# A decoder layer on one Trainium2 core: one copy frees the shared PSUM bank of cross-attention, its users are placed in other steps, context loads go to ScalarE's queue, and one-hot rows are made by wide operations

## The chip, the core and the metric

The kernel runs on one core of a Trainium2 chip. A core has TensorE (PE, matmuls and transposes), VectorE (DVE), ScalarE (ACT), GpSimd (POOL) and SyncE (SP, which here only issues DMAs). Each runs its own instructions in order, and they wait for one another through semaphores. SBUF and PSUM have 128 partitions, and PE writes only to PSUM. The metric is the device time of one execution in microseconds (us); lower is better.

## The reference

A pre-norm decoder layer in f32: `x` is (4, 512, 512) and the context (4, 512, 512).

```python
x = x + attention(layernorm(x), W_qkv, W_out, b_out)       # 16 heads of 32, rotary, window of 128
x = x + cross(layernorm(x), context, Wq, Wk, Wv)
x = x + experts(layernorm(x), router, gate, up, down)      # 64 experts, top 8, capacity 256

# cross: 32 heads of 16
q = rmsnorm(heads(x @ Wq.T)); k, v = heads(context @ Wk.T), heads(context @ Wv.T)   # interleaved in one kv
k = rmsnorm(k)
out = softmax(q @ k.T * 16 ** -0.5) @ v

# experts, the routing part
probs = softmax(xf @ router_weight); topw, topi = top_k(probs, 8); topw /= topw.sum()
pos = place of each (token, expert) pair among the tokens of its expert
```

## The kernel before

The 2048 tokens are 16 tiles of 128 (four batches, `T` = 4 tiles each), `D` = 512 is `C` = 4 pieces of 128. Three parts follow each other: self-attention (to about 460 us), `cross_attention()` (L625, to about 1086 us) and `experts()` (L1515). The change lies in the second.

Cross-attention is one walk over steps, `WALK`. Each engine's program is a loop over the same steps, and what it does in a step is given by functions that return step numbers (L773 to L815): `begin` (the first projection of a tile), `done`, `kn_step`, `x_step`, `stats_step`, `out_step`, `rn_step`, `rt_step`, `rp_step`, `pos_step`, `hot_step`. Steps 0 to 127 are attention, 32 for each batch: eight groups of four heads by four tiles of 128 keys. Steps -37 to -1 are a prologue that makes keys and queries of the first batch. Steps 128 to 141 finish the routing. Below, "step 8 of batch 1" is step 32 + 8.

In an attention step PE makes four score matmuls (`scores`, L1435, f32, 512 columns) into a PSUM `ring`, ACT takes their exponentials (L1035, two of 128x1024), and PE multiplies the previous step's by the values (`values`, L1447) into `xa_out`. Keys and queries of batch n are made while batch n-1 is attended to: eight tiles for each batch, four of the context (keys and values) and four of the input (queries). A tile's way:

- X: the input tile lies in `shared` (context, `cx`, two buffers, loaded by SP at L898) or is normalised by DVE into `xn` (L1126). PE turns it into the bank `b0` (`turn_x`, L1352). ACT copies the bank into `xh`, rounded to PE's fast f32 form (`high`, L1043); DVE subtracts `xh` from the bank and gets the rest, `xl` (`low`, L1193).
- Projection: in four steps (context) or two (query) PE multiplies `xh` and `xl` by the weights `wh` and `wl` (three products, L95 to L97), into `pr`. ACT takes squares (L1054), DVE reduces them (`mean_squares`, L1147; for batch 0 with further small operations up to a reciprocal, L1153) and copies out the raw heads (L1168). The root mean square is applied by DVE in batch 0 (`heads`, L1174 to L1185) and by POOL in the others (L997, L1000).
- KN: PE turns the normalised heads into `b0` (`turn_heads`, L1361), ACT and DVE split them into `hl[:, 0]` and `hl[:, 1]` (L1046, L1193; both lie in `stage`), and SP stores both to `turned` in DRAM (`store_turned`, semaphore `st_h`). When the batch's tiles are stored, `load_turned` (L925) loads them in the layout of `kT` and `qT`.

One PSUM bank, `b0`, carries all turns, in the order that `uses_at` gives for each step: OUT (every fourth step the finished group's output, which DVE copies to `oT`, L1295; PE turns it, L1455, and DVE divides by the row sum and adds, L1203 to L1209), KN, X, then for the routing of the batch before: LG (the logits of a tile, `project_route`, L1397, read by DVE at L1215), RT (the turn of a normalised tile, L1387, copied by DVE into `turned_x`, L1197) and POS (positions among the tokens of each expert, L1412). A user may write the bank when the one before has been read, which `s_free` counts (`bank_free`). In the last batch routing has banks of its own. In the loops the users of a step come behind scores and values on PE, and behind `take_values` on DVE.

When a batch's logits are there, DVE picks the top eight (`choose`), ACT takes exponentials of gates, and DVE computes each pair's place. From these `slots` (L1260 to L1278) makes one-hot rows for PE (`add_to_table`, L1422), which builds the table of tokens for each expert: for each of the 16 tiles `row_at` and `token_at`, 128 by 8 times 128 in f16. The first twelve tiles take sixteen operations of 128x128 (L1275, L1277), the last four three wide ones of 128x1024 (L1269, L1270, L1272). These tiles fall in the last batch and behind it.

## Time and profile before

| | |
|---|---|
| median of three runs | 1616.55 us (1614.88 to 1617.36) |
| profiled execution | 1621.8 us, span 1620.0 us, mean granted clock of PE 0.944 |
| busy, share of the span | PE 87%, DVE 63%, ACT 60%, POOL 47% |
| prologue of cross-attention | 475 to 558.2 us |
| steps of batches 0, 1, 2, 3 | start at 558.2, 680.6, 814.3, 943.7; the last ends near 1043 us |
| experts | from about 1086 us |

All times but the median come from one profiled execution. The share of the clock is relative to PE's full rate of 2.4 GHz; its other level is 1.2 GHz. A group row gives a line of the code, engine, operation, output and inputs, shape, then busy time and mean ns of one, then the idle time before them and what ended it. A row of waits names the operation that waited, and behind the arrow the one it waited for. A row of the timeline gives start, duration, engine, line and operation, and in brackets a wait before it. A row of the windows gives its bounds, then the busy time of PE, PE's weight loads, DVE, ACT and POOL, the granted clock, the busy share of the DMA engines and GB/s.

### The profile page before, as it was taken

What the parts mean: (1) busy time and instruction counts of PE and PEld (TensorE: products, weight loads), DVE (VectorE), ACT (ScalarE), POOL (GpSimd) and SP (SyncE); (2) the same over time, 40 slices, a digit from 0 to 9 for tenths busy, and PEclk for the clock granted to TensorE, in tenths of its full rate; (3) what the DMA queues carried; (4) which work ended last, traced back from release to release, by engine and by line L of the source; (5) the groups of instructions that cost most, each with busy time, mean ns of one, the idle gap of its engine ahead of it and who ended that gap; (6) DMA issues with size and microseconds to landing.
All of it is one profiled execution on the core that took longest, in us unless ns stands there. A gap on an engine that the chain in (4) does not pass through costs nothing. (4 is left out here: it accounts for less than half of the span.)

```text
span 1620.0 us, 27999 instructions
## 1 busy us (share of the span) xinstructions
PE 1403.3 (87%) x9603; PEld 1035.6 (64%) x9603; DVE 1026.3 (63%) x2044; ACT 972.0 (60%) x1969; POOL 759.5 (47%) x492
## 2 busy tenths in 40 slices
PE   3999999999867578988998878749999999999990
PEld 2777877777645334444444423238999999999980
DVE  4677676776535324343434568747888888888870
ACT  3666565665523346744754766527777777777760
POOL 2445454454400126334533600024777777777762
PEclk9999999999979889989999998859999999999995
DMA  9000000000022783680690491267999999999977
GB/s 335 2 20 21 27 14 28 15 27 21 8 94 69 125 135 69 109 187 29 110 203 27 95 139 44 65 195 207 297 297 298 296 299 298 297 294 290 303 154 129
DMA packets 133108, 229.78 MB, mean 142 GB/s; under 512 B 17865, under 2 KB 51145, under 8 KB 132496
## 3 DMA queue, kind: packets, MB, share of 16 engines
q1 hardware_dynamic: 103184, 154.98, 35.5%
q0 software_dynamic: 29248, 72.53, 20.0%
q8 instruction: 58, 0.95, 0.2%
q10 hardware_dynamic: 576, 0.98, 0.2%
q14 instruction: 42, 0.34, 0.1%
HBM read 163.78 MB, written 71.83 MB: 145 GB/s over the span
## 5 line engine op out<-in xcount | busy, mean ns | idle before, releaser
L1035 ACT ACTIVATE shared<-xa_ring 128x1024 f32<-128x1024 f32 x256 | 247.0, 1031 | 94.8 <-PE xa_ring L1435 94.6
L997 POOL TENSOR_TENSOR shared<-shared,xa_half 128x32 f32<-128x32 f32 x24 | 130.3, 5428 | 251.7 <-DVE shared L1158 251.7
L1602 POOL DMA_INDIRECT ex_xg<-xn,token x128 | 173.9, 1359 | 81.1 <-issue 61.5
L354 ACT ACTIVATE sa_prob<-sa_sc_ps,sa_nmax 128x256 f32<-128x256 f32 x256 | 117.8, 472 | 93.5 <-DVE sa_nmax L446 93.5
L300 POOL TENSOR_TENSOR sa_prob<-sa_prob,sa_rinv 128x1024 f32<-128x1024 f32 x64 | 121.1, 1893 | 95.6 <-DVE sa_rinv L459 95.6
L95 PE MATMUL ex_ba<-ex_xh,ex_wh 128*128 128x256 f32 x512 | 150.7, 294 | 3.7 <-DVE ex_xl L1716 3.7
L97 PE MATMUL ex_ba<-ex_xh,ex_wl 128*128 128x256 f32 x512 | 145.9, 285 | 0.0
L96 PE MATMUL ex_ba<-ex_xl,ex_wh 128*128 128x256 f32 x512 | 145.8, 285 | 0.0
L1447 PE MATMUL xa_out<-shared 128*17 128x512 f32 x1024 | 140.3, 621 | 0.5 <-ACT shared L1035 0.4
L1703 DVE TENSOR_TENSOR ex_wl<-shared,ex_wh 128x1024 fp32r<-128x1024 f32 (+1 forms) x128 | 116.9, 955 | 36.3 <-ACT ex_wh L1646 36.3
L1435 PE MATMUL xa_ring<-xa_qT,xa_kT 48*128 48x512 f32 x512 | 103.8, 473 | 12.8 <-ACT shared L1035 8.2
L1613 POOL DMA_INDIRECT out_dram<-ex_y,target x64 | 103.0, 1609 | 23.1 <-issue 23.1
L1613 POOL DMA_INDIRECT odd_sum<-ex_y,target x64 | 102.8, 1606 | 22.5 <-issue 19.2
L95 PEld LDWEIGHTS ex_ba<-ex_xh,ex_wh 128*128 128x128 f32 x512 | 98.6, 193 | 19.5 <-issue 19.5
L1646 ACT ACTIVATE ex_wh<-shared 128x1024 fp32r<-128x1024 f32 (+1 forms) x128 | 100.2, 831 | 17.1 <-PEq L1553 17.1
L446 DVE TENSOR_REDUCE sa_nmax<-sa_sc_ps 128x2 f32<-128x512 f32 x128 | 82.5, 686 | 27.1 <-PE sa_sc_ps L587 27.1
L96 PEld LDWEIGHTS ex_ba<-ex_xl,ex_wh 128*128 128x128 f32 x512 | 99.1, 193 | 0.0
L97 PEld LDWEIGHTS ex_ba<-ex_xh,ex_wl 128*128 128x128 f32 x512 | 98.9, 193 | 0.0
L287 POOL TENSOR_TENSOR sa_rot<-sa_t 128x512 f32<-128x512 f32 x32 | 47.0, 1467 | 97.5 <-DVE sa_t L414 97.5
L426 DVE CAST sa_kT<-sa_tn_ps 96x512 fp32r<-96x512 f32 x64 | 44.0, 687 | 73.8 <-PE sa_tn_ps L546 73.8
L1661 ACT ACTIVATE ex_sg<-ex_ba 128x256 f32<-128x256 f32 x64 | 24.5, 383 | 107.5 <-PE ex_bb L97 107.5
L1716 DVE TENSOR_TENSOR ex_xl<-ex_bx,ex_xh 128x512 fp32r<-128x512 f32 x128 | 82.5, 686 | 8.1 <-ACT ex_xh L1657 6.1
(223 smaller groups left out, 3929.6 us busy)
## 6 DMA issues: line engine op xcount, KB each, us to landing
shared<-in_L_ffn_gate_proj_dram SPq DMA_DIRECT2D x64, 384.0 KB, 5.8
shared<-in_L_ffn_up_proj_dram SPq DMA_DIRECT2D x64, 384.0 KB, 7.7
turned<-stage SPq DMA_DIRECT2D x64, 256.0 KB, 2.8
shared<-in_L_ffn_down_proj_dram SPq DMA_DIRECT2D x64, 256.0 KB, 5.1
xa_kT<-turned SPq DMA_DIRECT2D x96, 128.0 KB, 8.9
xa_qT<-turned SPq DMA_DIRECT2D x96, 128.0 KB, 11.5
shared<-in_L_ffn_down_proj_dram SPq DMA_DIRECT2D x64, 128.0 KB, 6.6
sa_x<-in_x_dram SPq DMA_DIRECT2D x16, 256.0 KB, 2.7
```

The source lines that it names most:

```text
L95: pe.matmul(out, hi_l(c), hi_r(c), start=(c == 0), stop=False)
L96: pe.matmul(out, hi_l(c), lo_r(c), start=False, stop=False)
L97: last = pe.matmul(out, lo_l(c), hi_r(c), start=False, stop=(stop and c == chunks - 1))
L300: pool.tensor_tensor(prob[:, 4 * g:4 * g + 4, :], prob[:, 4 * g:4 * g + 4, :], rinv[:, 4 * g:4 * g + 4].unsqueeze(2).to_broadcast([P, 4, 2 ...
L354: act.activation(prob[:, h, :], sc_ps[p][:, i, :], ACT.Exp, bias=nmax[:, h:h + 1], accum_out=rsum[:, h:h + 1]).then_inc(s_ex[p], 1)
L997: pool.tensor_tensor(power[:, i], ms[:, i], half[:], ALU.pow).then_inc(s_pw, 1)
L1035: act.activation(prob[:, w % 2, 2 * i:2 * i + 2, :], ring[i][:], ACT.Exp, scale=D2 ** -0.5).then_inc(s_ex[i], 1)
L1435: last = pe.matmul(ring[u][:, i, :], kT[half, pair, kt * P:(kt + 1) * P], qT[half, pair, :], start=True, stop=True)
L1447: last = pe.matmul(out_ps[32 * i:32 * i + D2 + 1, :], v[:, b % 2, kt, 4 * g + i, :], prob[:, w % 2, i, :], start=(kt == 0), stop=(kt == T ...
L1602: pool.indirect_dma_start(out=xg[:, e % RING, j, :], out_offset=None, in_=xn3, in_offset=bass.IndirectOffsetOnAxis(token[:, at:at + 1], 0))\
L1613: pool.indirect_dma_start(out=odd_sum if e % 2 else out, out_offset=bass.IndirectOffsetOnAxis(target[:, at:at + 1], 0), in_=y[:, e % RING, ...
L1703: dve.tensor_tensor(lo, src, hi.bitcast(F32), ALU.subtract).then_inc(s_wl, 1)
```

## The change

1. **The bank is copied at once.** Users KN and X are read from `b0` by one DVE copy (`take`), into `hl[:, 1]` and `turned_x[:, 1]`; it frees the bank. ACT's `high` reads the copy, and DVE's `low` subtracts from the copy one step later, behind the first bank read of that step. It has a semaphore of its own, `s_low`, which the store of KN and the first projection of X now wait for. The copy of KN waits until the store of the KN before has landed, as `high` did.
2. **Users within a step.** On PE the first user of a step comes between scores and values, the second behind the values, others behind the projections. On DVE the first bank read comes ahead of the output copy.
3. **Users among steps.** X of batches 1 to 3 and the statistics come one step earlier. For the routing of batches 0 and 1, RT moves from steps 4, 8, 10, 14 of the next batch to 6, 10, 15, 22, LG from 8, 10, 14, 15 to 8, 12, 20, 24, and the positions from 19 to 28; choosing and gates move with these. Batches 2 and 3 keep their steps. RT of the first batches uses `turned_x[:, 0]` alone, and a routed tile t lies in `xn[:, t]`, where it was `(2 + t) % 4`; the waits for its buffers follow (also in `choose`, which now waits for the stores of tiles 2 and 3).
4. **Context loads** are issued by ACT, behind its `high`, and no longer by SP.
5. **One-hot rows** of the first twelve tiles are made by two wide comparisons and one product. `row1` holds 1 to 128 in f16 and lies in `target`; one more small operation in the prologue of the weights makes it.

```diff
@@ -768,6 +769,7 @@
         column = m.sb("column", [P, NT, TOPK], F16)
         row = m.sb("row", [P, NT, TOPK], F16)
         table = pr[:, 1, 0:P]
+        row1 = target[:].bitcast(F16)[:, 0:P]
...
@@ -783,10 +785,10 @@
             return done(n, j) + (3 if n == 0 else 4)
         def x_step(n, j):
-            return begin(n, j) - 1
+            return begin(n, j) - (1 if n == 0 else 2)
         def stats_step(n, t):
-            return begin(n, T) - 6 + t
+            return begin(n, T) - (6 if n == 0 else 7) + t
         def out_step(b, g):
             return STEPS * b + T * g + 5
@@ -795,13 +797,13 @@
             return STEPS * (b + 1) + (3 + t if b < B - 1 else 3)
         def rt_step(b, t):
-            return STEPS * (b + 1) + ((4, 8, 10, 14)[t] if b < B - 1 else 4)
+            return STEPS * (b + 1) + ((6, 10, 15, 22)[t] if b < B - 2 else (4, 8, 10, 14)[t] if b < B - 1 else 4)
         def rp_step(b, t):
-            return STEPS * (b + 1) + ((8, 10, 14, 15)[t] if b < B - 1 else 5 + t)
+            return STEPS * (b + 1) + ((8, 12, 20, 24)[t] if b < B - 2 else (8, 10, 14, 15)[t] if b < B - 1 else 5 + t)
         def pos_step(b):
-            return STEPS * (b + 1) + (19 if b < B - 1 else 9)
+            return STEPS * (b + 1) + (28 if b < B - 2 else 19 if b < B - 1 else 9)
         def sel_step(b):
             return pos_step(b) - 1
@@ -873,8 +875,11 @@
         def values_of(n, j, i):
             return banks_of(n, j)[i].rearrange("p (h d c) -> p h d c", d=D2, c=2)[:, :, :, 1]
-        def route_slot(t):
-            return (2 + t) % T
+        def route_turn(b, t):
+            return turned_x[:, t % 2 if b >= B - 2 else 0]
+
+        def copy_of(kind):
+            return turned_x[:, 1] if kind == "x" else hl[:, 1].bitcast(F32)
...
@@ -891,14 +896,8 @@
                     sp.wait_ge(s_xr, (n - 2) * T + t + 1)
                 sp.dma_start(xs[:, n % 2, t], x1[n * T + t]).then_inc(ld_x[n % 2][t], 16)
-            def load_context(n, t):
-                before = (n, t - 2) if t >= 2 else (n - 1, t + 2)
-                if before[0] >= 0:
-                    sp.wait_ge(s_b0, USE["x", *before] + 1)
-                sp.dma_start(cx[:, t % 2], context[n * T + t]).then_inc(ld_c[t], 16)
-
             def store_turned(n, j):
-                sp.wait_ge(s_free, FREE["kn", n, j] + 1)
+                sp.wait_ge(s_low, HIGH["kn", n, j] + 1)
                 for part in range(2):
                     sp.dma_start(turned[n % 2, j // T, part, :, j % T * P:(j % T + 1) * P].rearrange("(c p) t -> p c t", p=P),
                                  hl[:, part].bitcast(F32)).then_inc(st_h, 16)
...
@@ -1036,14 +1031,10 @@
             def high(kind, b, j):
-                u = (kind, b, j)
-                act.wait_ge(s_b0, USE[u] + 1)
+                act.wait_ge(s_free, FREE[kind, b, j] + 1)
                 if kind == "x":
                     at_least(act, s_pr, number(b, j) - 1)
-                    act.activation(xh[:, j % 2], b0[:], ACT.Copy).then_inc(s_high, 1)
-                else:
-                    at_least(act, st_h, 32 * number(b, j))
-                    act.activation(hl[:, 0], b0[:], ACT.Copy).then_inc(s_high, 1)
+                act.activation(xh[:, j % 2] if kind == "x" else hl[:, 0], copy_of(kind), ACT.Copy).then_inc(s_high, 1)
...
@@ -1068,6 +1059,12 @@
                 for t in range(T):
                     last = act.activation(gates[:, t], logits[:, t], ACT.Exp, bias=negative[:, t:t + 1])
                 last.then_inc(s_sum, 1)
+
+            def load_context(n, t):
+                before = (n, t - 2) if t >= 2 else (n - 1, t + 2)
+                if before[0] >= 0:
+                    act.wait_ge(s_b0, USE["x", *before] + 1)
+                act.dma_start(cx[:, t % 2], context[n * T + t]).then_inc(ld_c[t], 16)
...
@@ -1082,12 +1079,16 @@
                 for u in uses_at(w):
                     if u[0] in ("kn", "x"):
                         high(*u)
+                for n, t in at(lambda n, t: x_step(n - 1, T - 1) + 2, w, [(n, t) for n in range(1, B) for t in range(2)]):
+                    load_context(n, t)
+                for n, t in at(lambda n, t: x_step(n, t - 2), w, [(n, t) for n in range(B) for t in range(2, T)]):
+                    load_context(n, t)
...
@@ -1186,15 +1187,22 @@
                                              ALU.mult)
                 last.then_inc(s_kd, 1)
+            def take(kind, b, j):
+
+                dve.wait_ge(s_b0, USE[kind, b, j] + 1)
+                if kind == "kn":
+                    at_least(dve, st_h, 32 * number(b, j))
+                dve.tensor_copy(copy_of(kind), b0[:]).then_inc(s_free, 1)
+
             def low(kind, b, j):
                 dve.wait_ge(s_high, HIGH[kind, b, j] + 1)
                 hi, lo = (xh[:, j % 2], xl[:, j % 2]) if kind == "x" else (hl[:, 0], hl[:, 1])
-                dve.tensor_tensor(lo, b0[:], hi.bitcast(F32), ALU.subtract).then_inc(s_free, 1)
+                dve.tensor_tensor(lo, copy_of(kind), hi.bitcast(F32), ALU.subtract).then_inc(s_low, 1)
...
@@ -1268,15 +1276,15 @@
                     token_k, row_k = [a[:, i].rearrange("p k q -> p (k q)").rearrange("p (q k) -> p q k", k=TOPK) for a in (token_at, row_at)]
                     dve.tensor_tensor(token_k, from1k[:], column[:, n:n + 1].to_broadcast([P, P, TOPK]), ALU.is_equal).then_inc(s_col, 1)
                     dve.tensor_tensor(row_k, from1k[:], row[:, n:n + 1].to_broadcast([P, P, TOPK]), ALU.is_equal)
-                    dve.wait_ge(s_col, n - NT + T + 1)
+                    dve.wait_ge(s_col, n + 1)
                     dve.tensor_scalar(token_k, token_k, token1[:, n:n + 1], None, ALU.mult).then_inc(s_hot, 1)
                     return
-                for k in range(TOPK):
-                    dve.tensor_scalar(row_at[:, i, k], from1k[:, :, 0], row[:, n, k:k + 1], None, ALU.is_equal)
-                for k in range(TOPK):
-                    last = dve.tensor_scalar(token_at[:, i, k], from1k[:, :, 0], column[:, n, k:k + 1], token1[:, n:n + 1],
-                                             ALU.is_equal, ALU.mult)
-                last.then_inc(s_hot, 1)
+                places = row1.unsqueeze(1).to_broadcast([P, TOPK, P])
+                dve.tensor_tensor(token_at[:, i], places, column[:, n].unsqueeze(2).to_broadcast([P, TOPK, P]),
+                                  ALU.is_equal).then_inc(s_col, 1)
+                dve.tensor_tensor(row_at[:, i], places, row[:, n].unsqueeze(2).to_broadcast([P, TOPK, P]), ALU.is_equal)
+                dve.wait_ge(s_col, n + 1)
+                dve.tensor_scalar(token_at[:, i], token_at[:, i], token1[:, n:n + 1], None, ALU.mult).then_inc(s_hot, 1)
...
             for w in WALK:
+                for u in uses_at(w)[:1]:
+                    take_use(*u)
+                for u in uses_at(w - 1):
+                    if u[0] in ("kn", "x"):
+                        low(*u)
                 for b, g in at(out_step, w + 1, [(b, g) for b in range(B) for g in range(G)]):
                     take_values(b, g)
                 for n, j in at(lambda n, j: done(n, j) + 1, w, TILES):
                     if n == 0:
                         heads(j)
-                for kind, b, j in uses_at(w):
-                    if kind == "out":
-                        take_out(b, j)
-                    elif kind == "logits":
-                        take_logits(b, j)
-                    elif kind == "pos":
-                        take_positions(b)
-                    elif kind == "route":
-                        if b < B - 1:
-                            take_turned(b, j)
-                    else:
-                        low(kind, b, j)
+                for u in uses_at(w)[1:]:
+                    take_use(*u)
...
@@ -1366,7 +1382,7 @@
                 k = number(n, j)
                 pieces = C if j < T else 2
                 if step == 0:
-                    pe.wait_ge(s_free, FREE["x", n, j] + 1)
+                    pe.wait_ge(s_low, HIGH["x", n, j] + 1)
...
             for w in WALK:
                 if 0 <= w < STEPS * B:
                     scores(w)
+                for u in uses_at(w)[:1]:
+                    use(*u)
                 if 0 <= w - 1 < STEPS * B:
                     values(w - 1)
-                for kind, b, j in uses_at(w):
-                    if kind == "out":
-                        turn_out(b, j)
-                    elif kind == "kn":
-                        turn_heads(b, j)
-                    elif kind == "x":
-                        turn_x(b, j)
-                    elif kind == "logits":
-                        project_route(b, j)
-                    elif kind == "pos":
-                        positions(b)
-                    else:
-                        turn_route(b, j)
+                for u in uses_at(w)[1:2]:
+                    use(*u)
                 for n, j in TILES:
                     step = w - begin(n, j)
                     if 0 <= step < (C if j < T else 2):
                         project(n, j, step)
+                for u in uses_at(w)[2:]:
+                    use(*u)
```

DVE at a tile's boundary in the prologue, before (`stage` is the KN half in `hl`, `xa_xl` the half of X; the reduction group L1147 to L1153 belongs to the tile before that X):

```order
L1185 TENSOR_TENSOR stage<-xa_pr,shared 128x256 x2
L1193 TENSOR_TENSOR stage<-xa_b,stage 128x512
L1193 TENSOR_TENSOR xa_xl<-xa_b,xa_xh 128x512
L1147 TENSOR_REDUCE shared<-shared 128x32
L1150 TENSOR_SCALAR shared<-shared 128x32
L1151 TENSOR_SCALAR shared<-shared 128x32
L1153 RECIPROCAL shared<-shared 128x32
```

And after:

```order
L1195 COPY stage<-xa_b 128x512
L1195 COPY xa_turned_x<-xa_b 128x512
L1201 TENSOR_TENSOR stage<-stage 128x512
L1148 TENSOR_REDUCE shared<-shared 128x32
L1151 TENSOR_SCALAR shared<-shared 128x32
L1152 TENSOR_SCALAR shared<-shared 128x32
L1154 RECIPROCAL shared<-shared 128x32
L1201 TENSOR_TENSOR xa_xl<-xa_turned_x,xa_xh 128x512
L1175 TENSOR_TENSOR shared<-shared 128x32
```

The subtraction of X stood ahead of the reduction and now stands behind it; that of KN stands ahead of it still; two copies are new.

PE in step 8 of batch 1, from the scores to the first projection, before:

```order
L1435 MATMUL xa_ring<-xa_qT,xa_kT 128x512 x4
L1447 MATMUL xa_out<-shared 17x512 x4
L1361 MATMUL xa_b<-ident,stage 128x128 x4
L1352 MATMUL xa_b<-ident,shared 128x128 x4
L1397 MATMUL xa_b<-xa_rw,xa_turned_x 128x64 x4
L1387 MATMUL xa_b<-ident,xa_xn 128x128 x4
L95 MATMUL xa_pr<-xa_wh,xa_xh 128x512
```

And after:

```order
L1451 MATMUL xa_ring<-xa_qT,xa_kT 128x512 x4
L1377 MATMUL xa_b<-ident,stage 128x128 x4
L1463 MATMUL xa_out<-shared 17x512 x4
L1413 MATMUL xa_b<-xa_rw,xa_turned_x 128x64 x4
L95 MATMUL xa_pr<-xa_wh,xa_xh 128x512
```

KN (L1361, now L1377) moved ahead of the values (L1447, now L1463); X (L1352) and RT (L1387) have left the step, and LG (L1397, now L1413) stands alone behind the values.

DVE around step 8 of batch 0, up to the reading of OUT in step 9, before:

```order
L1108 BN_STATS xa_st<-stage 128x6
L1295 COPY xa_oT<-xa_out 128x512
L1193 TENSOR_TENSOR stage<-xa_b,stage 128x512
L1193 TENSOR_TENSOR xa_xl<-xa_b,xa_xh 128x512
L1147 TENSOR_REDUCE shared<-shared 128x32
L1158 TENSOR_SCALAR shared<-shared 128x32
L1168 COPY stage<-xa_pr 128x256 x2
L1108 BN_STATS xa_st<-stage 128x6
L1203 RECIPROCAL xa_rinv<-xa_b 128x16
L1205 TENSOR_TENSOR xa_scaled<-xa_b,xa_rinv 128x256
```

And after:

```order
L1195 COPY xa_turned_x<-xa_b 128x512
L1109 BN_STATS xa_st<-stage 128x6
L1195 COPY stage<-xa_b 128x512
L1201 TENSOR_TENSOR xa_xl<-xa_turned_x,xa_xh 128x512
L1303 COPY xa_oT<-xa_out 128x512
L1148 TENSOR_REDUCE shared<-shared 128x32
L1159 TENSOR_SCALAR shared<-shared 128x32
L1169 COPY stage<-xa_pr 128x256 x2
L1109 BN_STATS xa_st<-stage 128x6
L1211 RECIPROCAL xa_rinv<-xa_b 128x16
```

X's copy (L1195 to `xa_turned_x`) comes a step ahead of KN's (to `stage`), its subtraction (L1201) behind KN's copy; the subtraction of KN has moved behind OUT and is below this piece.

## Rows read from the trace of the kernel before

**Rows 1.** Busy time by engine, windows; the last columns are clock, DMA share, GB/s.

```profile
680.60:814.30 133.70, 118.15 (x677) 59.45 (x676) 57.02 (x136) 78.80 (x112) 55.19 (x23) 0.94 0.56 111
```

**Rows 2.** Waits of PE, 558 to 1043 us: total, times, longest.

```profile
PE xa_b L1352 <- DVE stage L1193: 12.3, 8, 1.5
...
PE xa_b L1352 <- DMA shared<-in_ctx_dram: 9.3, 1, 9.3
...
PE xa_b L1352 <- DVE xa_xn L1126: 6.4, 6, 1.2
...
PE xa_b L1397 <- DVE xa_xl L1193: 6.0, 4, 1.5
...
PE xa_b L1387 <- DVE xa_logits L1215: 5.0, 9, 1.7
...
PE xa_ring L1435 <- DMA xa_qT<-turned: 4.6, 2, 2.5
...
PE xa_pr L1422 <- DVE stage L1277: 4.0, 5, 1.0
...
PE xa_b L1387 <- DVE xa_xl L1193: 3.0, 2, 1.5
...
PE xa_b L1361 <- DVE xa_scaled L1205: 2.7, 3, 0.9
```

**Rows 3.** Busy time by engine, windows: steps 4 to 16 of batches 1 and 2.

```profile
694.40:765.50 71.10, 59.74 (x321) 32.75 (x320) 28.52 (x63) 33.03 (x45) 27.14 (x10) 0.88 0.40 103
...
828.10:897.00 68.90, 57.52 (x323) 31.50 (x322) 28.04 (x63) 32.92 (x45) 27.16 (x10) 0.90 0.38 99
```

**Rows 4.** Busy window in the last batch, then groups of DVE instructions by form.

```profile
948.20:995.00 46.80, 37.56 (x257) 16.73 (x256) 42.14 (x135) 24.89 (x26) 2.00 (x2) 0.88 0.65 112
...
L1703 DVE TENSOR_TENSOR ex_wl<-shared,ex_wh 128x1024 fp32r<-128x1024 f32 x64 | 78.5, 1226 | 36.3 <-ACT ex_wh L1646 36.3
...
L1277 DVE TENSOR_SCALAR stage<-xa_from1k,xa_column,xa_token 128x128 f16<-128x128 f16 x96 | 30.5, 391 | 0.0
...
L1275 DVE TENSOR_SCALAR stage<-xa_from1k,xa_row 128x128 f16<-128x128 f16 x96 | 24.7, 329 | 0.0
...
L1269 DVE TENSOR_TENSOR stage<-xa_from1k,xa_column 128x1024 f16<-128x1024 f16 x4 | 2.8, 688 | 0.8 <-PE xa_pr L1422 0.8
...
L1272 DVE TENSOR_SCALAR stage<-stage,xa_token 128x1024 f16<-128x1024 f16 x4 | 1.9, 478 | 0.0
```

**Rows 5.** Timeline of PE, step 4 of batch 1: start, us, engine, line.

```profile
696.09 0.66 PE L1361 MATMUL xa_b<-ident,stage 128*128 128x128 f32 x4
...
698.28 0.63 PE L1352 MATMUL xa_b<-ident,shared 128*128 128x128 f32 x4 [1.53 <-DVE stage L1193]
```

**Rows 6.** Timeline, prologue: DVE and PE at a tile's boundary.

```profile
493.05 0.69 DVE L1193 TENSOR_TENSOR xa_xl<-xa_b,xa_xh 128x512 fp32r<-128x512 f32 x1 [1.44 <-ACT xa_xh L1043]
...
493.80 0.50 PE L95 MATMUL xa_pr<-xa_wh,xa_xh 128*128 128x512 f32 x1
...
495.25 0.35 DVE L1153 RECIPROCAL shared<-shared 128x32 f32<-128x32 f32 x1
```

**Rows 7.** Timeline, end of the prologue: ACT, SyncE's queue, PE.

```profile
540.97 0.60 ACT L1046 ACTIVATE stage<-xa_b 128x512 fp32r<-128x512 f32 x1 [1.77 <-DMA turned<-stage]
...
545.60 0.60 ACT L1046 ACTIVATE stage<-xa_b 128x512 fp32r<-128x512 f32 x1 [4.03 <-DMA turned<-stage]
...
550.17 2.66 SPq L925 DMA_DIRECT2D xa_qT<-turned  x6
...
558.22 0.73 PE L1435 MATMUL xa_ring<-xa_qT,xa_kT 48*128 48x512 f32 x4 [2.52 <-DMA xa_qT<-turned]
```

**Rows 8.** Timeline, SyncE's queue: context for batch 1.

```profile
564.12 0.90 SPq L898 DMA_DIRECT2D shared<-in_ctx_dram  x2
```

**Rows 9.** Busy window; the share of the DMA engines is the last but one.

```profile
550.00:597.00 47.00, 34.26 (x170) 18.78 (x169) 7.43 (x16) 21.25 (x30) 12.98 (x4) 0.86 1.04 140
```

**Rows 10.** Timeline of PE: step 10 of batch 0 begins.

```profile
606.69 0.50 PE L1435 MATMUL xa_ring<-xa_qT,xa_kT 48*128 48x512 f32 x2
```

60 lines of the change are left out of this document (41 added, 19 removed).

## The prediction

> **What bounds the kernel now.** I first split the span into its stages. The change lies in cross-attention alone: a prologue from 475 to 558.2 us, then 128 steps up to 1043 us, 32 for each batch, the middle ones as in [rows 1]. A step is four score matmuls, four value matmuls, mostly six projection matmuls, and up to four *users* of the one PSUM bank `b0` (OUT, KN, X, LG and RT for outputs, key/query heads, inputs, logits and router turns). PE is busy for 118 of 134 us in a middle batch, ACT for 79 and DVE for 57. So PE's order is the path, and what counts is what PE waits for [rows 2]: a bank that DVE has yet to read, and once, for 9.3 us, a context tile. After such waits the granted clock falls from 2.4 to 1.2 GHz: it averages 0.88 and 0.90 over two stretches of some 70 us [rows 3]. In the last batch the projections are over and DVE is the bound: 42.1 of 46.8 us [rows 4].
>
> **Bank copied at once.** Now ACT reads the bank, DVE reads it again, and only then may PE write: two users in one step are 2.19 us apart at their starts, 1.53 of it waiting [rows 5]. After the change one DVE operation over the bank, 0.69 us [rows 6], frees it, and users stand apart or have the value matmuls between them, about 1 us. What goes, outside the last batch: 12.3 + 6.4 + 6.0 + 3.0 + 2.7, another 2.7 (the same wait on `scaled` by X) and 2.4 of the 5.0 us of the logits row [rows 2], 35.5 us. The 6.4 us (queries not yet normalised) go too, since that step now stands before a reduction that waits for PE. I take off 1.5 us for the wait at step 8, which belongs to the sum below: **-34.0**.
>
> **What the copy costs in the prologue.** DVE now subtracts (`low`) one step after the copy. For the prologue's inputs this puts `low` behind the reduction of the previous tile, which waits for ACT's squares and so for the end of that tile's projection. Before: `low` at 493.05, the next projection at 493.80, and the reduction only after it, with its last operation, a reciprocal, until 495.60 [rows 6]. After: 495.6 + 0.69 + 0.1 = 496.4, so 2.6 us idle at each boundary. The first costs 2.6 and 0.7 for the extra copy; the next two cost about 1.0 each, as other small waits fall in it; at the first normalised tile about 2.2 comes back, which leaves +3.0. The last three KN tiles go through one buffer: store landed, high, low, store, 4.6 us a turn (545.60 - 540.97 of high) [rows 7]. A turn now holds the copy as well, and between copy and `low` stand the next tile's head operations, 1.4 us. Working on from +3.3 at the last query tile, their stores leave at +5.3, +6.7 and +7.4. So the loads that start the steps (550.17 now) come at 557.6, and step 0 at 565.7 rather than 558.22.
>
> **Context on ScalarE's queue.** The 9.3 us wait [rows 2] is for a load issued at 564.12 behind the 30 loads of turned keys and queries [rows 8]. From ACT it is issued before them, and the wait goes, with some 1.8 us of half clock after it. But DVE's copy of KN(1,1) needs the store of KN(1,0) landed (both lie in `hl`), and that store is in the same queue behind all 42 loads. The DMA engines are full from 550 to 597 [rows 9]; 7.4 us later that is about 604. Without waits step 9 comes at 595.8, and its OUT turn needs that copy, then `low` and the copy of the output: 604.0 + 3 x 0.69 = 606.1. PE stands 9.6 us there. Step 10 starts at 608.9, with 1.8 of half clock 610.7, against 606.7 [rows 10]: **+4.0** for prologue and ten steps. The wait is not removed, it moves.
>
> **New waits in the steps.** KN stores now leave about 4 us later (copy, high, then `low` behind the next OUT) and DVE, not ACT, waits for their landing, with all its work queued behind. At step 8 of batches 1 and 2 the store sits behind the batch's loads: I get 2.3 and 1.5 us. At step 17 twelve key loads (12 x 1.02 us at the packed rate of [rows 9]: 46 transfers in 47 us, with issue 13.5) go ahead of the fourth KN store; the copy of the fifth waits until 22.0 us after step 17 starts while PE wants the bank at 18.5: 3.5 us in each of two batches. In batch 0 the output copy stands behind a `low` at step 24: 2.0. Choosing experts and positions moves to steps 27 and 28, where ACT's exponentials set the pace (those for the gates are no longer covered), and the positions' DVE work delays the output copy: 2.9 and 2.3. Small waits for the output copy, as OUT now precedes the values: 3 x 0.4. Sum **+19.2**.
>
> **Clock.** The two stretches lose 0.12 x 71.1 + 0.10 x 68.9 = 15.4 us [rows 3]. With the paired waits gone I expect two shorter falls per batch to remain, after the new waits, 3.4 us in each batch: 15.4 - 6.8 gives **-8.6**. Bounds: nothing, and -15.4.
>
> **Last batch.** A tile's sixteen small operations take (24.7 + 30.5) / 12 = 4.6 us; three wide ones replace them. No row shows the new layout. Bounds for a wide comparison: 0.69 us for the same shape with another repeated dimension, 1.23 us for the f32 subtraction of 128x1024, and 0.48 for the product [rows 4]. I take 1.23: the row at 0.69 reads both operands element by element, and here `column` repeats one value 128 times along the innermost dimension. That is 2.9 us a tile, 1.7 less. Seven tiles fall in the 46.8 us stretch: DVE falls from 42.1 to 30 us, and PE (37.6 us busy, some 2.8 of it lost to half clock) is next, so about 36.5 us: -10.3. In the remaining steps the 4.0 us of table waits [rows 2] shrink by 3.2 and the clock gives 2.5: -5.7. **-16.0**; with 0.69 us it is about 3 us more. If PE and ACT leave only half of it, -8: that is the other bound. The wait for queries at the batch's start (2.1 of the 4.6 us) is swallowed: **-2.1**.
>
> The Trainium skill (VectorE: DVE Perf Modes, What auto-detection actually checks) says that two 16-bit values go at once only where every tensor has step 1 or -1; here one has step 0. By that rule the wide comparisons run at the slow end and the batch gives -16; by the row of the same operation and type it would give -19. No run here shows which.
>
> **Sum.** +4.0 - 34.0 + 19.2 - 8.6 - 16.0 - 2.1 = -37.5 us. The profiled execution took 1621.8 us (span 1620.0), so 1584.3; the median of the runs is 5.2 below it, which gives **1579 us**. Nothing moves behind 1043 us.
>
> **Rivals.**
> - *The clock stays low.* Each new wait costs a full fall as the old ones did: +8.6, and the last batch's 5.3 us of clock too: 1593. For: falls follow waits in [rows 3]. Against: single waits in batch 0 cost none.
> - *The late store does no harm.* If the KN chain keeps its old times, 7.4 us of prologue and 10.8 us of store waits (2.3 + 1.5 + 3.5 + 3.5) go: 1561. Against: the order of DVE's rows.
> - *Respreading gives nothing.* DVE's in-order queue, with the copies (0.69 us x 16 a batch) and its waits for stores, hands PE as many waits as it takes away (34.0 lost, 8.6 of clock lost, 19.2 not paid twice): -37.5 + 23.4 = -14: 1602. For: DVE idles 5 us in one of the new waits.
> - *Slower than before.* Steps 16 to 26 hold five KN tiles. If copy, high, `low` one step later, store and landing become the period there, it is 0.69 + 0.60, some 3.6 until `low`, 0.69 and 3.3 (the 4.6 us turn of [rows 7] without its high and low): 8.9 us. Five take 44 us where the ten steps take some 31 without their waits: +13 in each of three batches, and +8 more where the key loads land: 1626. It decides from a period above 6 us per KN; the middle ones have two steps, about 7 us, and the third `low` slips behind an OUT. Against: only the fifth is bound in my steps.
>
> **How the numbers follow.** The forecast (1568 to 1590) has 0.45, low clock 0.20, harmless store 0.13, respreading for nothing 0.14, slower 0.08. I give 1557 to 1605 as range: it takes in the fast end of the wide operations beside the harmless store, and the third rival. About 0.2% (3.2 us) is what a measurement tells here: faster 0.91, same 0.02, slower 0.07.
>
> **What would show it.** In the profile after: prologue's end near 565 us, not 558; no wait for context; instead a wait of about 9 us of an OUT turn in step 9 with DVE's bank copy just before it; waits of the second user in a step below 0.3 us; a wait at RT in step 22 of batches 1 and 2; one-hot comparisons at 1.2 us; the last batch at 82 to 84 us. The forecast is wrong if step 0 is at 558 (then the prologue term falls), or if the batches still take above 125 us.

## The result, and the profile after

The changed kernel takes 1598.56 us (median of four runs, 1598.38 to 1599.97) against 1615.72 us before. The ratio is 0.9895, 95% interval 0.9875 to 0.9916: faster by 17.2 us, where 37 had been forecast. The profiled execution has a span of 1596.9 us, 23.1 less than that of before. All stages below come from these two executions. By stages (start of step 0, of step 96, of step 127, end of span):

| stage | before | after | change | in the prediction |
|---|---|---|---|---|
| prologue (first X to step 0) | 82.9 | 96.7 | +13.8 | +7.4 |
| steps 0 to 95 | 385.5 | 359.2 | -26.3 | -28.9 |
| steps 96 to 126 | 96.3 | 82.3 | -13.9 | -16.0 |
| from step 127 on | 580.1 | 583.2 | +3.2 | 0 |

Windows of the changed kernel: prologue, steps 0 to 9, the rest of batch 0, batches 1, 2 and 3, and the stretch to the first matmul of the experts. The columns are those of [rows 1].

```profile
475.40:572.10 96.70, 61.90 (x234) 46.78 (x234) 47.69 (x117) 24.07 (x50) 1.36 (x4) 0.81 0.38 98
572.10:615.80 43.70, 38.07 (x196) 18.20 (x196) 15.65 (x37) 24.31 (x34) 16.84 (x5) 0.88 0.92 134
615.80:690.00 74.20, 70.15 (x417) 31.86 (x416) 34.32 (x66) 52.16 (x66) 36.22 (x14) 1.00 0.43 92
690.00:816.40 126.40, 116.82 (x677) 57.61 (x676) 65.43 (x153) 79.23 (x112) 55.13 (x23) 0.96 0.61 123
816.40:931.30 114.90, 108.50 (x652) 51.68 (x651) 62.87 (x149) 76.85 (x108) 55.45 (x24) 0.99 0.55 117
931.30:1016.70 85.40, 77.35 (x573) 31.41 (x573) 59.81 (x115) 63.65 (x77) 4.18 (x6) 0.96 0.35 70
1016.70:1063.50 46.80, 20.61 (x97) 15.60 (x90) 22.52 (x64) 7.31 (x20) 7.05 (x8) 0.54 0.56 174
```

The same windows of the kernel before, for its prologue, batch 3 and the stretch behind it:

```profile
475.30:558.20 82.90, 57.24 (x230) 41.72 (x230) 36.68 (x98) 22.54 (x49) 1.39 (x4) 0.84 0.44 111
...
943.70:1042.90 99.20, 82.82 (x569) 32.80 (x573) 80.49 (x271) 63.47 (x76) 3.22 (x6) 0.90 0.36 61
...
1043.00:1086.60 43.60, 17.00 (x97) 12.27 (x89) 22.51 (x64) 7.31 (x20) 7.14 (x8) 0.64 0.59 188
```

Batch 1 went from [rows 1]'s 133.7 us and 0.94 of the clock to 126.4 and 0.96, and batch 2 from 129.4 and 0.95 to 114.9 and 0.99. The prologue went the other way. Steps 0 to 95 as one window, before and after:

```profile
558.20:943.70 385.50, 333.88 (x1945) 164.24 (x1945) 153.69 (x356) 232.75 (x321) 163.93 (x65) 0.95 0.58 108
```

```profile
572.10:931.30 359.20, 333.54 (x1939) 159.35 (x1939) 178.28 (x401) 232.55 (x320) 163.65 (x65) 0.97 0.59 116
```

PE's work in them is as long as it was (333.9 and 333.5 us, with a few records missing). What fell is its idle time, from 51.6 to 25.7 us.

PE's waits after, first in the prologue, then from step 0 to the end of the walk:

```profile
PE xa_ring L95 <- DVE xa_xl L1201: 12.7, 4, 4.2
PE xa_pr L95 <- DVE xa_xl L1201: 12.0, 5, 2.8
```

```profile
PE xa_ring L1451 <- ACT shared L1030: 11.3, 23, 1.4
PE xa_b L1471 <- DVE xa_oT L1303: 6.9, 4, 5.6
PE xa_b L1403 <- DVE stage L1195: 3.7, 2, 1.9
PE xa_b L1368 <- DVE xa_xn L1127: 3.3, 3, 1.6
...
PE xa_b L1377 <- DVE xa_turned_x L1195: 2.0, 1, 2.0
PE xa_b L1413 <- DVE xa_scaled L1213: 1.5, 2, 0.8
PE xa_b L1413 <- DVE stage L1195: 1.3, 1, 1.3
```

Most of [rows 2] is gone: the context wait of 9.3 us, the pairs (12.3, 6.0, 3.0), and half of the wait for queries (6.4, now 3.3). In the prologue the projection of each of the nine tiles, the first of the next batch among them, now waits 2.2 to 4.2 us for its `low`.

### The profile page after: what moved, and what is told of

Same layout as the page of the kernel before. It is cut to its first block and busy times, and to the rows that moved or that the text cites. A ratio compares the mean times of both kernels' runs of the same rounds, so it can differ in the third digit from the quotient of the medians.

```text
span 1596.9 us, 27909 instructions
## 1 busy us (share of the span) xinstructions
PE 1405.2 (88%) x9603; PEld 1037.1 (65%) x9603; DVE 1041.5 (65%) x1953; ACT 973.5 (61%) x1969; POOL 760.2 (48%) x492
## 3 DMA queue, kind: packets, MB, share of 16 engines
q0 software_dynamic: 29248, 72.53, 20.3%
## 5 line engine op out<-in xcount | busy, mean ns | idle before, releaser
L1463 PE MATMUL xa_out<-shared 128*17 128x512 f32 x1024 | 138.2, 612 | 0.4 <-ACT shared L1030 0.4
L1636 POOL DMA_INDIRECT out_dram<-ex_y,target x64 | 103.0, 1609 | 23.1 <-issue 23.1
L1636 POOL DMA_INDIRECT odd_sum<-ex_y,target x64 | 102.8, 1606 | 22.5 <-issue 19.2
L1451 PEld LDWEIGHTS xa_ring<-xa_qT,xa_kT 48*128 48x128 f32 x512 | 41.8, 187 | 90.4 <-ACT shared L1030 44.9
```

The costliest lines, as they stand in the source:

```text
L1451: last = pe.matmul(ring[u][:, i, :], kT[half, pair, kt * P:(kt + 1) * P], qT[half, pair, :], start=True, stop=True)
L1463: last = pe.matmul(out_ps[32 * i:32 * i + D2 + 1, :], v[:, b % 2, kt, 4 * g + i, :], prob[:, w % 2, i, :], start=(kt == 0), stop=(kt == T ...
L1636: pool.indirect_dma_start(out=odd_sum if e % 2 else out, out_offset=bass.IndirectOffsetOnAxis(target[:, at:at + 1], 0), in_=y[:, e % RING, ...
```

## The experiments

All times are medians; the ratio to the kernel before comes from runs on the same chip, and has its interval. The medians of the kernel before beside them were 1616.8 to 1619.0 us. Single executions of one kernel differ by up to 16 us, so a stage is compared in the traces and the whole by the ratio.

### Low ahead of the reduction, in the prologue

```diff
                 for u in uses_at(w - 1):
-                    if u[0] in ("kn", "x"):
+                    if u[0] in ("kn", "x") and w > 0:
                         low(*u)
...
                 for u in uses_at(w)[1:]:
                     take_use(*u)
+                for u in uses_at(w):
+                    if u[0] in ("kn", "x") and w < 0:
+                        low(*u)
                 for n, j in at(done, w, TILES):
                     mean_squares(n, j)
```

> The changed kernel, but in the prologue of cross-attention (steps below 0) DVE's low stands in the same step as the copy, ahead of the reduction, as in the kernel before; from step 0 on nothing differs. Theory: the prologue got 13.9 us longer because every X waits for the reduction of the tile before (seven waits of the first projection for the low of X, 2.2 to 4.2 us, with half clock behind each). Then these waits return to about 1.4 us or vanish, step 0 comes at 560 to 563 us instead of 572.1, and the whole kernel takes 1587 to 1590 us instead of 1598.6. Rival: the chain of the last KN tiles (copy, high, low, store landed) sets the end of the prologue whatever the first tiles do; then step 0 comes no earlier than 567 and the kernel takes 1593 us or more.

1585.6 us, ratio 0.9796 (0.9758 to 0.9834). Step 0 comes at 564.2 us, 88.1 us after the first X, where it was 96.7. The prologue as a window, and the waits of its projections:

```profile
476.10:564.20 88.10, 57.77 (x234) 42.30 (x234) 48.20 (x117) 23.88 (x50) 1.37 (x4) 0.85 0.42 108
```

```profile
PE xa_pr L95 <- DVE xa_xl L1201: 6.4, 5, 2.2
...
PE xa_ring L95 <- DVE xa_xl L1201: 2.6, 3, 1.5
```

24.7 us of these waits are 9.0 now, and the clock is back from 0.81 to 0.85. Others return: 9.5 us for the normalised inputs, as in the kernel before, and 5.7 for heads, where it was 3.5. PE's idle time in the prologue falls by 4.5 us (34.8 to 30.3) and its busy time by 4.1 (61.9 to 57.8), so about half of the gain is clock. Only the order of `low` was changed, so it is the cause of 8.6 of the prologue's 13.8 us. The size differs between executions: the six traces with `low` behind the reduction and KN copied as in the changed kernel have prologues of 96.7 to 101.0 us, the changed kernel's own being the shortest, and the two with `low` ahead of it 88.1 and 86.0. Step 0 at 564.2 lies between the two expectations: 5.2 us remain, and the longest wait that does is one of 5.2 us for the heads of the last KN tiles. The whole span is 11.6 us shorter; batch 3 and what is behind it give 5.2 of that, and nothing was changed there.

### Wide one-hot rows alone

The kernel before with part 5 of the change and nothing else; `row1` is made in the prologue of the weights as there.

```diff
-                for k in range(TOPK):
-                    dve.tensor_scalar(row_at[:, i, k], from1k[:, :, 0], row[:, n, k:k + 1], None, ALU.is_equal)
...
+                dve.tensor_tensor(row_at[:, i], places, row[:, n].unsqueeze(2).to_broadcast([P, TOPK, P]), ALU.is_equal)
...
```

> The kernel before with the one-hot rows of the first twelve tiles by three wide operations, and nothing else changed. Theory: in the changed kernel the last batch gained 13.9 us from step 96 to step 127, mostly by this part; alone it takes 10 to 14 us off the last batch (96.3 us from step 96 to step 127 before) and the kernel takes 1602 to 1606 us. Rival: the last batch gained by the other parts (X's and the output copy's waits gone, clock), and this part alone gives at most 6 us, since PE and ACT were close to binding: 1610 us or more.

1607.0 us, ratio 0.9926 (0.9901 to 0.9950). Batch 3, from step 96 to the end of step 127:

```profile
939.90:1026.40 86.50, 78.50 (x569) 32.08 (x573) 59.90 (x115) 63.26 (x76) 4.18 (x6) 0.94 0.36 68
```

99.2 us are 86.5, where the whole change reaches 85.4. DVE's 80.5 us of work became 59.9, and PE with 78.5 us is now the busier engine. By the ratios this part alone gives 12 of the change's 17 us, and the other four parts together 5. The time lies just above the theory's 1602 to 1606, the gain in the last batch within its 10 to 14.

### Context on ScalarE's queue alone, and back on SyncE's

The first kernel is the one before with

```diff
-                    sp.wait_ge(s_b0, USE["x", *before] + 1)
-                sp.dma_start(cx[:, t % 2], context[n * T + t]).then_inc(ld_c[t], 16)
...
+                    act.wait_ge(s_b0, USE["x", *before] + 1)
+                act.dma_start(cx[:, t % 2], context[n * T + t]).then_inc(ld_c[t], 16)
...
```

> The kernel before with only the context loads moved from SP's queue to ACT's. Theory: the 9.3 us wait for context in step 4 goes, and since ACT, not DVE, waits for the landing of a KN store here (ahead of its copy of KN in step 8), a wait of PE takes its place there: KN(1,0) is stored behind the loads, which land at about 596 us, while KN(1,1) is wanted at step 8, about 586 us. So I expect a wait of 8 to 10 us at step 8 and the same time within 3 us, 1613 to 1618 us. Rival: the store lands in time, since the DMA queues serve it beside the loads, and the kernel gains the whole wait and its clock, 9 to 11 us: 1605 us.

1614.9 us, ratio 0.9976 (0.9962 to 0.9989), within the theory's range; the profiled run is 8.9 us above the median. Against the kernel before the wait of step 4 goes, and step 8 gets one for the bank, since ACT's copy of KN(1,1) waits for the store of KN(1,0). PE in step 8:

```profile
597.47 1.09 PE L1352 MATMUL xa_b<-ident,shared 128*128 128x128 f32 x4 [5.71 <-DVE stage L1193]
```

The wait is 5.7 us, not 8 to 10. Steps 0 to 9 take 45.5 us, where they took 48.5. Now the opposite: the changed kernel with the same lines the other way round, the loads on SP.

> The changed kernel with the context loads back on SP's queue. Theory: the moved load only trades one wait for another, since the landing of KN(1,0), behind all loads of the first batch, sets step 9 in any case. So the wait for context returns at step 3 (8 to 10 us), the 5.6 us at step 9 goes to zero, step 10 comes 2 to 5 us later than 615.8, and the kernel takes 1600 to 1604 us. Rival: the two waits add up (14 us in these ten steps), step 10 comes 9 us later and the kernel takes 1607 us or more.

1613.4 us, ratio 0.9976 (0.9957 to 0.9996), 15 us slower than the changed kernel by the medians and 13 by the ratios. Waits of PE from step 0 on:

```profile
PE xa_b L1368 <- DMA shared<-in_ctx_dram: 18.6, 3, 12.3
```

My theory fell: step 9 loses its wait as it said (3.8 us), but the context waits more than fill that place. X comes a step earlier in the changed kernel, so the same load is 3 us later for it (12.3 us for 9.3), and the next two batches wait too, which they did not before. Steps 0 to 9 take 51.4 us, not 43.7, and steps 0 to 95 take 374.1, not 359.2. The time is the rival's, but the two waits do not add up. The prologue of this execution was 4.3 us longer as well, at lower clock; the profiled run is 4.6 us above the median of its ten.

### Routing at its old steps

```diff
-            return STEPS * (b + 1) + ((6, 10, 15, 22)[t] if b < B - 2 else (4, 8, 10, 14)[t] if b < B - 1 else 4)
+            return STEPS * (b + 1) + ((4, 8, 10, 14)[t] if b < B - 1 else 4)
```

The steps of LG and POS are put back likewise.

> The changed kernel with the routing of batches 0 and 1 at the steps of the kernel before (RT 4, 8, 10, 14; LG 8, 10, 14, 15; POS 19), everything else as changed. Theory: with the bank copied at once, and the second user behind the values, the respreading removes only the waits of third users (step 8) and adds its own: step 22 (3.6 and 4.1 us longer in batches 1 and 2 with the clock) and steps 28 and 29 (4.2 and 2.0 us). Without it batches 1 and 2 take 238 to 244 us together, where they take 241.3, and the kernel stays within 4 us of 1598.6. Rival, as the prediction had it: the respreading carries much of the gain on the bank (34 us with the copies), and without it batches 1 and 2 take 250 us or more, the kernel 1607 us or more.

1601.9 us, ratio 0.9899 (0.9867 to 0.9931): by the ratios no difference from the changed kernel. In the traces batches 1 and 2 take 247.1 us where they took 241.3, between the two expectations. Steps 22, 28 and 29 of the two batches give back some 13 us, but step 8 takes 13.5 and 9.2 us, where it took 10.2 and 4.7. In batch 1 PE waits there for DVE's copy of X, and DVE has waited for an input tile:

```profile
726.55 1.09 PE L1377 MATMUL xa_b<-ident,stage 128*128 128x128 f32 x4 [4.59 <-DVE xa_turned_x L1195]
```

```profile
725.12 0.69 DVE L1109 BATCH_NORM_STATS2 xa_st<-stage 128x6 f32<-128x512 f32 x1 [9.03 <-DMA stage<-x]
```

The experiment on the last quarter's loads below says why that tile is late. In batch 1 the same step took 13.4 us in the first experiment too, which has the routing of the changed kernel, so at most batch 2's part can be put down to the old steps. The respreading is worth 0 to 6 us.

### KN copied to a buffer of its own, alone and with the first edit

In batches 0 and 1 `turned_x[:, 0]` is free. DVE's copy then needs no landing; ACT's `high` waits for it.

```diff
-            return turned_x[:, 1] if kind == "x" else hl[:, 1].bitcast(F32)
+            return turned_x[:, 1] if kind == "x" else turned_x[:, 0] if n < 2 else hl[:, 1].bitcast(F32)
...
```

> The changed kernel, but the copies of KN of the first two batches go to turned_x[:, 0], which no one uses until step 38, and so do not wait for the landing of the store before; ACT's high waits for it instead. Theory: the wait of 5.6 us at OUT of step 9 exists because DVE's whole queue stands behind the landing of KN(1,0); with the copy free of it, OUT is read at once and the wait and its half clock go, 5.6 + 1.5 us, and the last KN tiles of the prologue come 2 to 4 us earlier: 1588 to 1592 us. Rival: the wait only moves, from DVE's copy to DVE's low one step later (it needs ACT's high, which waits for the same landing), and ACT's exponentials stand behind high as well: PE waits for them just as long, and the kernel stays at 1596 to 1600 us.

1594.6 us, between the two expectations; the ratio of 0.9857 (0.9823 to 0.9891) can't be told from the changed kernel's 0.9895 (0.9875 to 0.9916). In the traces the prologue is 4.3 us shorter, and step 9 takes 5.9 us for 11.0. Part of it comes back at once. In batch 0:

```profile
PE xa_b L1372 <- DVE xa_xn L1129: 2.2, 1, 2.2
PE xa_pr L95 <- DVE stage L1171: 2.0, 1, 2.0
```

> The changed kernel with both mends: low in the prologue ahead of the reduction, and KN of the first two batches copied to turned_x[:, 0]. The first alone brought step 0 to 564.2 us, the second to 567.3, from 572.1. Theory: the first removes the waits of the projections of X, the second the DMA landing from DVE's queue in the last KN tiles; they act on different pieces, so step 0 comes at 559 to 562 us, the wait in step 9 stays at 2 us or less, and the kernel takes 1580 to 1584 us. Rival: both only remove slack of one chain, three KN stores one behind the other, so step 0 stays at 563 to 565, and the kernel takes 1585 us or more.

1584.7 us, ratio 0.9813 (0.9779 to 0.9848), just outside the theory's 1580 to 1584; its four runs lie between 1575.0 and 1590.0. In the trace the prologue takes 85.7 us and step 0 comes at 560.4, as the theory has it. The medians can't tell it from the first edit alone.

### The last quarter's loads behind the KN store

```diff
-                    if w == STEPS * n:
+                    if w == STEPS * n + 6:
                         for side in range(2):
                             load_turned(n, 3, side)
```

> The changed kernel, but SP issues the twelve loads of the last quarter of each batch's keys and queries at step 6 of the batch, not at its step 0, so behind the store of the next batch's first KN (step 4). Theory: that store lands late because these twelve loads and, in batches 1 and 2, the stores of the outputs stand ahead of it. Without them it lands some 12 us earlier: the wait of 5.6 us at step 9 of batch 0 goes (11.0 us to about 3.8), step 8 of batch 1 falls from 10.2 to 5 to 6 us, and the kernel takes 1585 to 1590 us instead of 1598.6. Rival: the store is late because of the thirty loads issued at the end of the prologue alone; then step 9 keeps most of its wait, step 8 of batch 1 keeps its 10 us, and the kernel takes 1596 us or more.

1593.6 us, ratio 0.9837 (0.9809 to 0.9865). The store of KN(1,0) in the changed kernel, DVE's wait for its landing, and then the store and DVE's copy in this one:

```profile
593.83 0.93 SPq L902 DMA_DIRECT2D turned<-stage  x2
```

```profile
609.15 0.69 DVE L1195 COPY stage<-xa_b 128x512 f32<-128x512 f32 x1 [9.40 <-DMA turned<-stage]
```

```profile
595.26 0.93 SPq L902 DMA_DIRECT2D turned<-stage  x2
596.23 3.09 SPq L924 DMA_DIRECT2D xa_kT<-turned  x6
...
603.73 0.69 DVE L1195 COPY stage<-xa_b 128x512 f32<-128x512 f32 x1 [2.54 <-PE xa_b L1377]
```

Step 9 takes 3.8 us for 11.0: its wait was this landing. Step 8 of batch 1 takes 4.7 for 10.2, by another way. In the changed kernel SP issues the stores of batch 0's output behind the twelve loads; the first lands 19.4 us later, at 717.69, and only then may SP load the next input tile into the same buffer. DVE's statistics wait for that tile, and the copies of X and KN stand behind them:

```profile
698.25 2.27 SPq L929 DMA_DIRECT2D out_dram<-stage  x4
...
717.71 0.33 SPq L897 DMA_DIRECT2D stage<-x  x1
```

```profile
720.82 0.70 DVE L1109 BATCH_NORM_STATS2 xa_st<-stage 128x6 f32<-128x512 f32 x1 [6.29 <-DMA stage<-x]
```

With the loads moved the first output store lands 8.7 us after its issue, and DVE finds the tile there. So 12.7 us are gone from two steps, but steps 0 to 95 as a whole take 359.6 us, where they took 359.2. The kernel gains 5 us by the medians and 9 by the ratios; the 3.8 us that its trace gains lie in batch 3 and behind the walk. Step 22 takes 1.5 to 2.2 us more in each of three batches. Step 11 of batches 0 and 2 each takes 3 us more, since the queries are not normalised yet. DVE waits there for a deviation that stands in GpSimd's queue behind a power of 5.4 us:

```profile
607.71 5.43 POOL L992 TENSOR_TENSOR shared<-shared,xa_half 128x32 f32<-128x32 f32 x1 [8.18 <-DVE shared L1159]
...
614.24 0.20 POOL L984 TENSOR_TENSOR xa_ve<-xa_mv,xa_eps 128x4 f32<-128x4 f32 x1
```

### Key loads split

```diff
                         load_turned(n, 0, 0)
+                    if w == kn_step(n, T - 1) + 3:
                         load_turned(n, 1, 0)
```

> The changed kernel, but of the twelve key loads that SP issues in step 17 of batches 0 to 2 six are issued two steps later, behind the store of the fourth query or key tile's KN (step 18). Theory (the term of 7.0 us in the prediction's sum): the wait of PE for the bank in step 22, 1.8 and 1.9 us with half clock behind it, is the landing of that store behind twelve loads, since DVE's copy of the next KN waits for it. With six loads ahead it lands in time; step 22 falls from 5.7 and 7.3 us to 3.3 us in batches 1 and 2, and the kernel gains 4 to 7 us: 1592 to 1595 us. Rival: the landing is not what is late, but DVE's other work in steps 20 and 21 (output copy, subtractions); then step 22 stays and the kernel takes 1597 us or more.

1587.1 us, ratio 0.9816 (0.9794 to 0.9838), more than expected. Step 22 with RT, in the changed kernel and in this one (batch 1):

```profile
783.26 0.63 PE L1403 MATMUL xa_b<-ident,xa_xn 128*128 128x128 f32 x4 [1.83 <-DVE stage L1195]
```

```profile
778.76 0.66 PE L1404 MATMUL xa_b<-ident,xa_xn 128*128 128x128 f32 x4
```

The step takes 3.8 us in both batches, for 5.7 and 7.3. Batches 1 and 2 lose 5.7 us, as expected. Batch 0 loses 3.4. Another 5.5 us of the span go in batch 3 and behind the walk, where nothing was changed, and those differ between executions.

### All four edits

> All four edits together on the changed kernel: low ahead of the reduction in the prologue, KN of the first two batches copied to turned_x[:, 0], the last quarter's loads at step 6, and the key loads split. Theory: they act at four different places (prologue 11.7 us, step 9, step 8 of batch 1, step 22 twice), so they add up to 22 to 28 us: 1571 to 1577 us. Rival: as the bank's waits go, ACT's exponentials and PE's clock set the pace and the gains overlap; 1580 us or more.

1571.4 us (1569.6 to 1572.9), ratio 0.9716 (0.9697 to 0.9736): 27 us faster than the changed kernel, as expected, and the fastest of the study. Steps 0 to 95 as one window:

```profile
561.70:902.60 340.90, 327.07 (x1941) 155.95 (x1941) 178.64 (x401) 232.71 (x320) 164.22 (x65) 0.99 0.62 122
```

359.2 us at 0.97 before these edits, and PE is busy in 96% of it now.

### The copies alone

The changed kernel with three parts undone together: routing at its old steps, context on SP, small one-hot operations. The order of users within a step and the earlier X stay, so "the copies" here are the copies with these two.

```diff
-            return STEPS * (b + 1) + (28 if b < B - 2 else 19 if b < B - 1 else 9)
+            return STEPS * (b + 1) + (19 if b < B - 1 else 9)
...
-                act.dma_start(cx[:, t % 2], context[n * T + t]).then_inc(ld_c[t], 16)
+                sp.dma_start(cx[:, t % 2], context[n * T + t]).then_inc(ld_c[t], 16)
...
-                dve.tensor_tensor(row_at[:, i], places, row[:, n].unsqueeze(2).to_broadcast([P, TOPK, P]), ALU.is_equal)
+                for k in range(TOPK):
+                    dve.tensor_scalar(row_at[:, i, k], from1k[:, :, 0], row[:, n, k:k + 1], None, ALU.is_equal)
...
```

> Of the change only the bank copies (take, low one step later), the order of users within a step, and X one step earlier; the routing of batches 0 and 1 at its old steps, context on SP, one-hot rows by the old small operations. Theory: alone these take 34 us of bank waits away and put nearly all of it back: 14 us of prologue, a context wait that is 3 us longer because X comes a step earlier (12.3 us), and waits for the landing of KN stores in DVE's queue. Put together from the other runs (context back on SP cost 15, old routing steps 3, the one-hot rows are worth 11.5), the kernel should take 1620 to 1630 us, slower than before or equal. Rival: the parts overlap, and the copies alone keep a third or more of their 34 us: 1605 us or less.

1627.6 us, ratio 1.0068 (1.0043 to 1.0093): slightly slower than before, as expected. Its prologue, and its longest waits from step 0 on:

```profile
475.60:574.00 98.40, 62.27 (x234) 46.69 (x234) 47.72 (x117) 24.08 (x50) 1.33 (x4) 0.81 0.37 94
```

```profile
PE xa_b L1367 <- DMA shared<-in_ctx_dram: 21.3, 3, 13.6
```

The bank waits are gone here too (batches 1 and 2 take 243.1 us for 263.1), and yet it loses: 15.5 us in the prologue and 7.1 in batch 0, and the last batch gains nothing.

The same with `low` ahead of the reduction in the prologue, as in the first experiment:

> The kernel e12_copies_only with low ahead of the reduction in the prologue. Theory: the prologue gives back 8 us of waits and 4 to 5 of half clock, as in the first experiment, so 10 to 13 us less than e12_copies_only, 1608 to 1618 us. Rival: the context wait swallows it, since its loads stand behind the same thirty loads, which start earlier by the same amount; no: they shift together with step 0, so if less than 5 us come through, the cause of the prologue's price isn't the order of low.

1617.3 us, ratio 0.9986 (0.9965 to 1.0007), so as fast as before. Step 0 comes at 561.1 us for 574.0, and of these 12.9 us 10.3 arrive in the median. The order of `low` is the price of the prologue in this setting too.

## Why the prediction was wrong

The side was right and the time lay in the range, but the gain was half of the forecast. Of the 19.6 us between 1579 and 1598.6, 14.4 are in the trace (37.5 less 23.1) and 5.2 are the distance of one execution from its median.

- **Prologue, +7.4: failed.** It measured +13.8, the largest miss. The mechanism was as described: `low` behind the reduction. The first boundary was also costed rightly (2.6 us idle, and 2.4 measured). The step that failed is the sum over the tiles behind it: 1.0 each for the next two, "as other small waits fall in it", then 2.2 coming back at the first normalised tile, and +3.3 at the last query tile. In the trace the first projections of the second, third and fourth tile come 2.5, 5.1 and 7.1 us later than before, counted from the first X, where 3.3, 4.3 and 5.3 were forecast; the first normalised tile gives nothing back (+8.3), and at the last query tile it is +11.9. Before and after:

```profile
511.10 0.50 PE L95 MATMUL xa_pr<-xa_wh,xa_xh 128*128 128x512 f32 x1
...
533.85 0.47 PE L95 MATMUL xa_ring<-xa_wh,xa_xh 128*128 128x512 f32 x1
```

```profile
519.48 0.50 PE L95 MATMUL xa_pr<-xa_wh,xa_xh 128*128 128x512 f32 x1 [2.43 <-DVE xa_xl L1201]
...
545.83 0.50 PE L95 MATMUL xa_ring<-xa_wh,xa_xh 128*128 128x512 f32 x1 [4.18 <-DVE xa_xl L1201]
```

Other waits do fall in it (9.5 us for normalised inputs are gone), but the nine of the projections are 24.7 us, where the projections waited 2.8. The chain of the last KN tiles, forecast to add 4.1 to the 3.3, added only 1.9. And the clock stood in the sum only for the steps. PE's idle time in the prologue grew by 9.1 us (25.7 to 34.8), and its busy time for the same matmuls by 4.7 (57.2 to 61.9), at a clock of 0.81 for 0.84. The first boundary shows both:

```profile
488.37 0.80 PE L95 MATMUL xa_ring<-xa_wh,xa_xh 128*128 128x512 f32 x1 [2.42 <-DVE xa_xl L1201]
488.97 0.63 PE L96 MATMUL xa_ring<-xa_wl,xa_xh 128*128 128x512 f32 x1
489.39 0.63 PE L97 MATMUL xa_ring<-xa_wh,xa_xl 128*128 128x512 f32 x1
```

The distance of the starts is 0.42 us here, at 1.2 GHz; just ahead of the wait, at 2.4 GHz, it is 0.24:

```profile
484.61 0.40 PE L96 MATMUL xa_pr<-xa_wl,xa_xh 128*128 128x512 f32 x1
484.85 0.40 PE L97 MATMUL xa_pr<-xa_wh,xa_xl 128*128 128x512 f32 x1
```

- **Steps 0 to 9: right in kind, half in size.** The context wait was replaced by one at OUT of step 9, with DVE's copy just before it, as forecast; 5.6 us, not 9.6. Step 0 came 6.4 us later than forecast and the landing (609.06) only 5, which is 1.4 of the difference; steps 0 to 8 took 32.7 us, where 30.1 had been taken, which is 2.6. That the store stands behind the last twelve loads was shown by moving them.
- **Bank waits, -34.0: near.** They are gone but for 3.3 us of the queries and 2.8 of the logits, and steps 0 to 95 gave 26.3 of 28.9 us. But the copies alone make the kernel slower. The copies pay only with the context moved, which the prediction had at +4.0 with the wait "moved". Taken back it costs 13 to 15 us, for X's earlier step makes SP's loads late in three batches. The prediction never costed the parts against each other.
- **New waits, +19.2: about right.** Step 22 waited 1.8 and 1.9 us instead of 3.5 each, and with half clock behind took 2.5 and 4.1 us more; splitting the loads removed it. Steps 28 and 29 took 6.2 us more in the two batches together (5.2 forecast). Step 8 waited 3.3 us in batch 1 (2.3 forecast) and not at all in batch 2 (1.5), and that the first is near is luck: it was not DVE's wait for a KN store, as the prediction has it, but its statistics' wait for an input tile. Partly by this step batch 1 took 126.4 us, above the 125 that the prediction had named as a sign of being wrong.
- **Clock, -8.6: right by the granted clock, not seen in the time.** Over steps 0 to 95 the loss by the clock went from 0.05 x 385.5 = 19.3 to 0.03 x 359.2 = 10.8 us, 8.5 less. But PE was busy for 333.9 us before and 333.5 after, so the 26.3 us are nearly all waiting (25.9 less). That the total of these steps came out near the forecast is in part luck: the terms without the clock add up to 20.3 us less, and PE's work didn't shrink. How much of the half clock before fell in waits stays open.
- **Last batch, -16.0: near.** -13.9. A wide comparison takes 1.21 us, as taken:

```profile
L1285 DVE TENSOR_TENSOR stage<-target,xa_row 128x1024 f16<-128x1024 f16 x12 | 14.6, 1216 | 0.0
L1283 DVE TENSOR_TENSOR stage<-target,xa_column 128x1024 f16<-128x1024 f16 x12 | 14.6, 1213 | 0.0
```

PE is busy for 77.4 of the 85.4 us there and DVE for 59.8, so I expect little from the end at 0.69 us; no run here has it. This agrees with what the prediction quoted from the Trainium skill (VectorE: DVE Perf Modes, What auto-detection actually checks): of the two forms the one whose innermost step is 0 in one operand ran at the slow end. The fast form [rows 4], 0.69 us, repeats values of `column` too, but along the outer dimension, with a step of 1 innermost; the prediction was wrong to say that it reads both operands element by element.

- **"Nothing moves behind 1043 us": failed by 3.2 us.** The same 32 matmuls of the last batch's logits, before and after:

```profile
1055.04 3.75 PE L1397 MATMUL xa_ring<-xa_rw,xa_turned_x 128*128 128x64 f32 x32
```

```profile
1028.79 6.93 PE L1413 MATMUL xa_ring<-xa_rw,xa_turned_x 128*128 128x64 f32 x32
```

Nothing was changed there; the clock of the stretch behind the walk is 0.54 for 0.64. In the traces of the twelve experiments this piece takes 3.75 us once, 4.1 to 4.3 seven times and 6.93 four times. What decides it stayed open.

- **The base.** The profiled execution of before was 5.2 us above its median, and I took that off the forecast as if the changed kernel had the same excess. Its own profiled run was at its median, so the difference of the traces (23.1) is larger than that of the medians (17.2), and the two must not be mixed.
- **Rivals.** "The clock stays low" came true in part: in steps 0 to 95 PE's work is as long as before, though the granted clock rose, but in batch 3 the clock rose from 0.90 to 0.96 and PE's work fell by 5.5 us. "Respreading gives nothing" was near the measured time (1602) but for another reason: its own experiment gives 0 to 6 us for the respreading, and the time was lost in the prologue. "The late store does no harm" is refuted by 5.6 us in step 9 and the waits of step 22. "Slower than before" got the side of the copies alone, but not their mechanism: they lose in the prologue and by the context wait, and batches 1 and 2, where a period of KN tiles would show, get 20 us shorter.
